# A DLRM interaction tower on one core: one-hot ring of eight units, one row buffer per gather slot, and layer three in column tiles

## What is computed

```python
e = jnp.stack([tbl_0[ids[:, 0]], ..., tbl_26[ids[:, 26]]], axis=1)      # 2048 x 27 x 128
dot = jnp.einsum('bnd,bmd->bnm', e, e)
z = dot[:, c, r]                                  # r, c = tril_indices(27, k=-1): 351 pairs
h = jnp.concatenate([z, dense_ctx], axis=1)       # 367
h = jnp.maximum(h @ W_top1 + b_top1, 0.0)         # 512
h = jnp.maximum(h @ W_top2 + b_top2, 0.0)         # 256
y = h @ W_top3                                    # 2048 x 1
```

## Time and profile before

| | |
|---|---|
| median of 3 runs | 572.7 us (572.4 to 577.95) |
| the profiled execution | 572.74 us, its span 570.9 us |
| mean granted TensorE clock in it | 0.848 of full speed |
| PE busy | 419.2 us (73%), 4118 matmul records |
| DVE busy | 232.5 us (41%) |
| ACT busy | 147.5 us (26%) |
| POOL busy | 253.0 us (44%) |
| DMA | 45.97 MB, 81 GB/s on the mean |

### The profile page before, as it was taken

How to read it: one execution, slowest core, us unless ns; L and a number is a source line. 1 busy time by engine, 2 the same in 40 slices (tenths; PEclk the granted TensorE clock), 3 DMA queues, 4 the chain that set the end, 5 groups by cost and what they waited for, 6 DMA issues and landing times.

```text
span 570.9 us, 10250 instructions
## 1 busy us (share of the span) xinstructions
PE 419.2 (73%) x4118; PEld 367.1 (64%) x4118; DVE 232.5 (41%) x730; ACT 147.5 (26%) x310; POOL 253.0 (44%) x269
## 2 busy tenths in 40 slices
PE   3411567867786896779896887858978688689887
PEld 3311566846775785658684775747867587578676
DVE  6511685524562262532462433433336225354200
ACT  3210241212221331223121331222312223124542
POOL 6777454446554443642545336254444453450000
PEclk9755588869797896978788898787979789799998
DMA  8943261234223421413215132052211431133130
GB/s 202 230 119 86 74 202 33 84 79 105 60 78 90 86 60 28 127 45 77 64 29 148 26 77 68 22 139 47 77 36 52 120 82 55 38 100 66 37 68 1
DMA packets 69280, 45.97 MB, mean 81 GB/s; under 512 B 53443, under 2 KB 57795, under 8 KB 69233
## 3 DMA queue, kind: packets, MB, share of 16 engines
q1 hardware_dynamic: 59255, 27.82, 20.4%
q0 software_dynamic: 8384, 17.19, 11.6%
q10 hardware_dynamic: 1594, 0.31, 0.3%
HBM read 39.53 MB, written 5.76 MB: 79 GB/s over the span
## 4 chain that ended last, share of the span: by engine, by line
PE 63%; issue 14%; another core or an unknown queue 11%; DVE 6%; DMA 2%; ACT 2%; SPq 1%; ACTq 0%; DVEq 0%
PE lookup_ps L558 33%; PE gram_ps L587 13%; PE layer_ps L604 7%; PE gather_ps L543 5%; DVE one_hot L833 5%; PE layer_ps L616 4%; PE layer_ps L624 1%; DMA ids_all<-lookup_ids 1%; DVE table_lo L840 1%; DMA emb<-tbl 1%; ACT z L735 1%; DMA z<-gram_dram 1%; SPq L357 1%; ACT h_rest L735 0%
## 5 line engine op out<-in xcount | busy, mean ns | idle before, releaser
L511 POOL DMA_INDIRECT rows<-tbl,index x256 | 246.4, 962 | 256.3 <-PE gather_ps L543 160.8
L833 DVE TENSOR_SCALAR one_hot<-ids_all,row_number 125x256 fp32r<-125x256 int32 x688 | 208.3, 366 | 295.0 <-remote 151.7
L558 PE MATMUL lookup_ps<-one_hot,table_hi 125*128 125x256 f32 x680 | 208.9, 332 | 86.3 <-issue 43.0
L558 PEld LDWEIGHTS lookup_ps<-one_hot,table_hi 125*128 125x128 f32 x680 | 145.6, 214 | 100.4 <-issue 65.0
L558 PE MATMUL lookup_ps<-one_hot,table_lo 125*128 125x256 f32 x680 | 193.7, 309 | 17.0 <-issue 16.7
L558 PEld LDWEIGHTS lookup_ps<-one_hot,table_lo 125*128 125x128 f32 x680 | 146.9, 216 | 26.4 <-issue 26.1
L587 PE MATMUL gram_ps<-emb 128*52 128x54 f32 x2048 | 84.4, 231 | 37.7 <-issue 35.4
L587 PEld LDWEIGHTS gram_ps<-emb 128*52 128x52 f32 x2048 | 69.8, 142 | 54.0 <-issue 47.2
L330 ACT COPY gram<-gram_ps 128x432 f32<-128x432 f32 x64 | 33.2, 518 | 193.9 <-remote 161.8
L697 ACT ACTIVATE emb<-lookup_ps 128x256 f32<-128x256 f32 x85 | 35.0, 412 | 83.8 <-remote 40.8
L686 ACT ACTIVATE emb<-gather_ps 128x512 f32<-128x512 f32 x64 | 38.9, 608 | 63.7 <-PE gather_ps L543 46.4
(11 more groups left out here) (40 smaller groups left out, 107.5 us busy)
## 6 DMA issues: line engine op xcount, KB each, us to landing
ids_all<-lookup_ids SPq DMA_DIRECT2D x43, 256.0 KB
gram_dram<-gram SPq DMA_DIRECT2D x62, 87.8 KB
emb<-tbl SPq DMA_DIRECT2D x11, 448.0 KB
rows<-tbl,index POOLq DMA_INDIRECT x256
z<-gram_dram SPq DMA_DIRECT2D x14, 117.0 KB
ids_all<-lookup_ids SPq DMA_DIRECT2D x7, 128.0 KB
z<-gram_dram SPq DMA_DIRECT2D x7, 91.0 KB
emb<-w SPq DMA_DIRECT2D x3, 192.0 KB
```

What stands on the lines that cost most here:

```text
L511: pool.indirect_dma_start(rows[k][:, j * DIM:(j + 1) * DIM], None, tables[f], bass.IndirectOffsetOnAxis(index[p][:, h, f:f + 1], 0)).then_ ...
L558: last = nc.tensor.matmul(lookup_ps[lookup_bank(c, p, k)], table[:, k, row, :], one_hot[u % UNIT_RING][:, r, :], start=(row == 0 and table ...
L833: last = nc.vector.tensor_scalar(one_hot[u % UNIT_RING][:, r, :], table_ids, row_number[0:LOOKUP_PARTS, row:row + 1], None, ALU.is_equal)
```

## The change

Three things are changed.

- `UNIT_RING` is 8 instead of 4. Since 44 units a chunk are no multiple of 8, the ring is indexed by the running number of the unit over all chunks.
- There are 4 row buffers instead of 8, one for each slot, which both halves use. `ROWS_FREE` is 4 instead of 8: slot n waits until slot n - 4 is transposed.
- Layer three is computed in 4 column tiles of 64 samples, whose results lie on the partitions 0, 32, 64 and 96 of PSUM. ACT copies 128 x 64 instead of 1 x 256 values, and the store takes 4 partitions of 64.

```diff
-UNIT_RING = 4
+UNIT_RING = 8
...
-        rows = [sbuf(f"rows{i}", [P, len(SLOTS[i % len(SLOTS)]) * DIM]) for i in range(N_GATHERS)]
+        rows = [sbuf(f"rows{i}", [P, len(SLOTS[i % len(SLOTS)]) * DIM]) for i in range(len(SLOTS))]
...
+        Y_TILES = 4
+        Y_COLS, Y_STEP = CHUNK // Y_TILES, P // Y_TILES
...
-            return Tower(z_sb, h1_sb, [h2_one, h1_sb[0]], h1_more[0:1, 0, :])
+            return Tower(z_sb, h1_sb, [h2_one, h1_sb[0]], h1_more[:, 0, 0:Y_COLS])
...
-        rows_in = [semaphore(f"rows_in{k}") for k in range(N_GATHERS)]
+        rows_in = [semaphore(f"rows_in{g}") for g in range(len(SLOTS))]
...
-        ROWS_FREE = N_GATHERS
+        ROWS_FREE = len(SLOTS)
...
                         pool.indirect_dma_start(
-                            rows[k][:, j * DIM:(j + 1) * DIM], None, tables[f],
-                            bass.IndirectOffsetOnAxis(index[p][:, h, f:f + 1], 0)).then_inc(rows_in[k], 16)
+                            rows[g][:, j * DIM:(j + 1) * DIM], None, tables[f],
+                            bass.IndirectOffsetOnAxis(index[p][:, h, f:f + 1], 0)).then_inc(rows_in[g], 16)
...
-                pe.wait_ge(rows_in[k], (c + 1) * 16 * len(SLOTS[g]))
+                pe.wait_ge(rows_in[g], (c * HALVES + k // len(SLOTS) + 1) * 16 * len(SLOTS[g]))
...
-                                                one_hot[u % UNIT_RING][:, r, :],
+                                                one_hot[(units_before(c) + u) % UNIT_RING][:, r, :],
...
-                    last = nc.tensor.matmul(layer_ps[0][0:1, 0:CHUNK], w3_sb[:, k:k + 1], to.h2[k],
-                                            start=(k == 0), stop=(k == o2_tiles - 1))
+                    for j in range(Y_TILES):
+                        last = nc.tensor.matmul(layer_ps[0][j * Y_STEP:j * Y_STEP + 1, 0:Y_COLS], w3_sb[:, k:k + 1],
+                                                to.h2[k][:, j * Y_COLS:(j + 1) * Y_COLS],
+                                                start=(k == 0), stop=(k == o2_tiles - 1))
...
-                nc.scalar.activation(to.y, layer_ps[0][0:1, 0:CHUNK], ACT.Copy).then_inc(y_ready, 1)
+                nc.scalar.activation(to.y, layer_ps[0][:, 0:Y_COLS], ACT.Copy).then_inc(y_ready, 1)
...
-              act.dma_start(y_out[bass.ds(c * CHUNK, CHUNK), :].rearrange("b o -> o b"),
-                              to.y).then_inc(y_stored, 16)
+              act.dma_start(y_out[bass.ds(c * CHUNK, CHUNK), :].rearrange("(j b) o -> j (b o)", j=Y_TILES),
+                              to.y[0:P:Y_STEP, :]).then_inc(y_stored, 16)
```

## The result

The changed kernel takes 552.8 us (median of 4 runs, 548.8 to 558.5). The kernel before, run beside it, takes 575.1 us (4 runs, 572.4 to 578.0). The ratio is 0.959, with a 95% interval of 0.948 to 0.969. So it is faster by some 4%, where I had forecast 560 us, that is 2%. The medians take all runs, the ratios only the runs within 1.5% of a kernel's fastest, so the two needn't divide to the same number. Its profiled execution took 550.25 us, with a span of 548.4 us, and it is this one that I set against the 572.74 us (span 570.9 us) of before.

A forecast was written before the change was run, and what follows sets the result against it. TensorE was taken as busiest, held up by POOL's gather bursts through late messages and a lower clock. From 572.74 us, -20.0 + 11.5 + 3.0 - 7.7 + 1.3 - 1.0 = -12.9 gave 560 us, range 549 to 572 us.

The forecast's parts named there:

- Rival 3: Stalls come from something coinciding with gathers, as instruction supply; neither end moves, ring and layer three remain: 564 us, chance 0.06.
- The start: POOL's first burst falls from 42 to 26 gathers, ending 20.0 us earlier: -20.0 us; ring's delay there +1.3 us.
- The bound of -22: Largest gain allowed for the shorter first burst at the start; the other bound was -8 us.
- The term of +1.3 us for the ring: At the start DVE makes eight units of chunk 1 before the last three `table_low`: +1.3 us, bounds 0 and +2.5.
- One mark: Sign to look for at the start: PE's transposition 0.1 comes before 30 us.
- The last half: From 7.0 to 7.3, slots 7.4 to 7.7 are now gathered, as in chunk 6's half: +11.5 us.
- Behind 7.3: Last burst slows the gram matmuls, transposition 7.4 3.5 us later, partly covered by z's load: +3 us, bounds 0 and +6.
- The ring: DVE eight units ahead saves half of PE's 15.4 us one-hot waits after the start: -7.7 us, bounds 0 and -15.4.
- Layer three: Column tiles save 3.9 us over 8 chunks, less 2.9 for extra records: -1.0 us, bounds -4 and +6.
- the term of +2.9 us for twelve more records in a burst: Layer three's 12 more records per chunk push out unit matmuls when a burst fills: +2.9 us, at most +8.4.
- Rival 1: Tables, ids or `table_low` set the start's pace when POOL pauses; half the 20 us is lost: 570 us, chance 0.16.
- Rival 2: The ring pays in full: PE's lost 15.4 us all come back and some bursts are passed: 552 us, chance 0.14.

The follow-up runs named there:

- its two variants: Changed kernel with one gather of four in chunk 4, one sample's store of four in chunk 5: 371.2 us; changed kernel with 7.4 to 7.7 gathered early: 374.6 us.
- the gated start: Kernel before, eight buffers kept, but POOL waits for the transposition four slots back in chunks 0 and 1: 375.6 us, ratio 1.0026, on chip 14.
- the early tail: Changed kernel with rows for 7.4 to 7.7 gathered early into id buffers, without loads and one-hots behind the last chunk: 374.6 us, ratio 0.999, chip 14.

## Why the prediction was right, and where its terms were not

**The cause.** That bursts of gathers hold TensorE and its messages up was read from the earlier trace rows and is now shown, within one execution: the chunk without most of its gathers takes 43.6 us, its neighbours 64 to 67 us, and the one with few stores 65.7 us. Nor is it the amount of data moved: the short chunk moved 77 GB/s, its neighbours 71 GB/s. Rival 3, the supply of instructions, loses by its own mark, since both ends moved. The pages speak against it as well: the queue that fetches instructions moved 33 blocks on the first chip and on chip 14 (packets, MB, share of 16 engines over the span):

```profile
q8 instruction: 33, 0.54, 0.4%
```

```profile
q8 instruction: 33, 0.54, 0.6%
```

With spans of 570.9 and 373.4 us both shares come to an estimated 1.1 us a block, so a block took no longer where PE stalled.

What isn't shown is how a gather does it. Issuing on POOL, the packets and the messages of their completion were always taken away together. What I had not seen, and could not from one trace, is that the chip decides whether gathers do this at all. The forecast of -2% is one for the kind of chip that the profile came from, where 4% and 2% were measured. On chips 5 and 14 the changed kernel itself wasn't run; its two variants there took 371.2 and 374.6 us against 375.2 and 374.8 us, which leaves of this change at most the tiles' 1%.

**The start, forecast -20.0 + 1.3, measured -25.1 us.** What is off is the step "POOL has the 6 extras, four slots, and slot 0.4: 26 gathers". I had counted on transposition 0.0 being visible just as POOL came to slot 0.4, and took that as hardly a pause. POOL came to it at 32.2 us, had nothing to issue for 4.09 us, and DVE recovered around that pause. So the first burst was 22 gathers. DVE's first run of eight, at 38.34 us, is 25.0 us ahead of the run of six in the earlier trace rows, and from there to transposition 1.0 both kernels take the same time, 48.5 and 48.6 us. That is the whole of the start's gain.

In the kernel with the buffers alone the burst was 26 gathers and ended at 39.2 us, just as forecast, and its start was as short (87.1 us). DVE there (start us, us, what, idle before):

```profile
40.29 0.62 DVE L833 TENSOR_SCALAR one_hot<-ids_all,row_number 125x256 fp32r<-125x256 int32 x2 [2.92 <-remote]
...
41.96 2.52 DVE L833 TENSOR_SCALAR one_hot<-ids_all,row_number 125x256 fp32r<-125x256 int32 x8
```

Its run of eight begins at 41.96 us, the 42 us of the forecast, 2.8 us behind the burst, where the earlier trace rows have 5.2 us (58.1 to 63.33 us). So 21.4 of its 24.8 us lie ahead of that point, 2.4 of them from the shorter recovery, which I had left as it was; for the other 3.4 us no row gives a reason.

The bound of -22 rested on the same step and was too narrow. The term of +1.3 us for the ring, the eight units ahead of the last three `table_low`, shows nowhere: with the ring the start is 4.2 and 1.4 us shorter on chip 2, not longer. One mark was missed: transposition 0.1 didn't come before 30 us but at 39.6 us, since PE waited 12 us for a one-hot of DVE's, late by the same message. It comes 11.4 us earlier than in the earlier trace rows, not 21.

**The last half, forecast +11.5, measured +9.6 us,** and 10.8 to 11.6 us on chip 2, against the same 21.5 us. The comparison of two equal stretches in the earlier trace rows was the best step of the prediction: it needed no model of the stall, only that the one stretch would become like the other.

**Behind 7.3, forecast +3, measured +6.6 us.** The timeline of the result shows the step as it was drawn, some 43 gram matmuls at full speed and then handfuls, up to transposition 7.4 at 511.4 us. 8.7 us pass from 7.3 to 7.4, where it was about 5 us (531.8 to 536.8 us): +3.7 us, as forecast (3.5). What failed is "a part is covered, since the stretch waits for z anyway". Nothing was covered: from 7.4 to 7.7 it takes 5.8 us rather than 3.7, and 0.8 us more behind 7.7. The granted clock gives the reason for the first of the two. From 7.4 to 7.7, after and before:

```profile
511.40:517.20 5.80, 5.47 (x77) 4.81 (x77) 0.00 (x0) 2.90 (x6) 0.00 (x0) 0.59 0.00 0
```

```profile
536.80:540.50 3.70, 3.35 (x79) 2.92 (x77) 0.00 (x0) 2.77 (x5) 0.00 (x0) 1.00 0.28 82
```

No gather is left in this stretch, and PE is busy in both, but behind the stalled grams the clock is at 0.59 of full speed, where it was at 1.00. I had ended the cost of the burst with PE's recovery and put the clock behind it at nothing. The bound of +6 was just too low here; on chip 2 the stretch behind 7.3 is 42.3 to 44.4 us against 39.1 us, within it. Rows for 7.7 were not late: PE waited 0.35 us at that transposition, for ACT, as in the earlier trace rows.

**The ring, forecast -7.7 us, measured -3.8 and -6.2 us.** The direction of the step is right (half of the waits is all that can be kept), and one mark of it is wrong. I wrote that "issue" stays near 70 us; it rose to 90.5 us. The wait for a one-hot goes, PE runs further into the burst, and there it stands in "issue" instead. A wait that lies inside a stall isn't worth its length. The tool for judging it was there: three of the waits in the earlier trace rows stood at the end of bursts of eight.

**Layer three, forecast -1.0 us, measured -4.1 us by itself on a chip without the stall,** which is past the bound of -4, and -4.7 and -7.1 us in six chunks on chip 2. The chain entry is 0.34 us for 16 records, 0.021 us each, where I had taken 0.0285 us from the gram banks. The larger error is the term of +2.9 us for twelve more records in a burst, which no run shows: the six chunks between 1.0 and 7.0 gain 4.7 to 7.1 us on chip 2, more than the 3.7 us of the tiles' own time, and not less. ACT's wait for layer three is shorter too, 5.6 us before and 1.8 us after over seven chunks. Why the gain exceeds the own time is not shown; single traces differ by as much. The rule that a change of tiling mode drains TensorE, weighed in the prediction from the Trainium skill (TensorEngine Tiling (Array Packing), Key Properties), would with the 0.17 us of the earlier trace rows have made layer three worth nothing. The tiles-only run puts it at -4.1 us over the program: if there is a drain, it is no larger than what is left between that and 8 x 0.61 = 4.9 us.

**The sum.** -25.1 - 13.6 + 9.6 + 6.6 = -22.5 us, where I had -12.9. Of the 9.6 us between, 6.4 are the start, 4.9 the steady part (tiles and ring; some 4 us of it stand in the kernel with the buffers alone too, 394.6 against 398.4 us on another chip, and aren't explained), 1.9 the last half, and the end gives 3.6 back. Rival 1 was wrong in its sign: tables and ids were ready when POOL paused. Rival 2's 552 us is the time that was measured, but not its mechanism: PE's 15.4 us did not come back in full, the start did more. That the total stayed inside the range is in part luck: the start went past its bound of -22 us and the end past its bound of +6 us, and the two errors partly cancel. The ends of the range were summed loosely as well: rival 2 with the start's bound gives 550 us, not 549, and rival 1 with the dearer end 573 us, not 572.

## What to carry to other kernels

When a wait labelled "issue" or "remote" comes in groups, look at what another engine does at just those times, and price it by two equal stretches of the same program, one with and one without it; such a comparison forecast its term within 2 us, while the terms put together from single steps were off by 4 to 6. When one engine's work holds the others up, the time at which it issues can matter more than how much it issues: with fewer buffers the start of this kernel was 25 us shorter on a chip that stalls, as POOL was stopped where others had work to do, while its end became dearer. And a chip that doesn't stall can't test a theory of the stall: put the suspect and its control into different chunks of one program, so that each execution says itself which kind of chip it ran on.

## What the runs showed of the hardware

- The same program takes 374.4 to 375.5 us on chips 14 and 5, and 558.0, 561.3 and 575.1 us on chip 10, chip 2 and the chip of the first runs. In a trace of the first kind PE is busy 92% of the span at a mean granted clock of 0.98, in one of the second 73% at 0.85. Where hardly a gather is left, behind 7.3, the two traces agree within 0.1 us in 39.
- On the second kind TensorE mostly runs some 45 to 65 matmuls into a burst of GpSimd's indirect DMAs at full speed, and then falls to one or a few in each 0.7 to 1.2 us, while VectorE and ScalarE go on up to 10 us late or more. With one gather in four left, a chunk goes from 63.9 to 66.8 us down to 43.6 us, and the clock back to 1.00. On the first kind 262 gathers in a row, one each 1.25 us, slow nothing that can be seen: a chunk takes 42.0 us with 31.9 us of POOL's work in it and with 7.7 us.
- From the end of the first burst to DVE's next run of six or more instructions it took 5.2 us after 42 gathers, 1.7 to 3.1 us after 26 (three kernels), and 3.2 to 6.1 us after 22, in the changed kernel with the next burst already begun. A rule by the burst's length doesn't come out of this.
- Behind a stalled stretch the clock stays low for a while: 0.59 from 7.4 to 7.7, without a gather, against 1.00 before the change, and 77 matmul records took 5.8 us where 79 had taken 3.7 us. In the 5.4 us ahead of it PE had been busy for 2.3 us.
- Sixteen fp32 matmuls of 64 columns in four column tiles take 0.34 us in the chain, four of 256 columns in one tile 0.95 us.

What stays open: in what the chips differ; by which way a gather reaches TensorE; whether recording the profile has a part in the stall, since every time here is that of a recorded execution, and the trace of the same kernel holds 8398 semaphore events on chip 14 and only 3801 on the first chip (a releaser without an event is called "remote"); what the gated start and the early tail would do on a chip that stalls, where they were not run; and how the 11 us of ring and tiles together divide between them.
